# Four-layer residual block on one core: the next group's filters prepared across two superblocks, their root as a power on GpSimd

## The reference

```python
x = x + ddf(_gn(x))        # layer 0: decoupled dynamic 3x3 filter
x = x + v * sigmoid(q . mean(k))   # layer 1, on _gn(x)
x = x + conv3x3(_gn(x), ternary(weight)) + bias
x = x + softmax(Q^T K) V   # layer 3: attention over 3136 pixels, on _gn(x)
```

```python
sf = einsum('bchw,nc->bnhw', x, ws) + bs
sf = (sf - sf.mean(2)) / (sf.std(2, ddof=1) + 1e-10) * (GAIN / K)
out[c,i,j] = sum over taps of x[c,i+u,j+v] * cf[c,tap] * sf[tap,i,j]
```

## Time and profile before

| | us |
|---|---|
| median of 3 runs | 1942.02 (1940.48 to 1942.21) |
| the profiled execution | 1941.18 |
| its span, first to last instruction | 1939.4 |
| mean granted TensorE clock | 0.92 |

### The profile page before, as it was taken

One profiled execution on the slowest core, in us unless ns is written; L12 is line 12 of the kernel. 1 busy time (PEld: TensorE's weight loads), 2 busy tenths in 40 slices (PEclk: granted clock), 3 DMA queues, 4 the chain that ended last, 5 costly groups with the idle time before them and its releaser, 6 DMA issues.

```text
span 1939.4 us, 35957 instructions
## 1 busy us (share of the span) xinstructions
PE 1673.0 (86%) x10840; PEld 829.7 (43%) x10840; DVE 1257.6 (65%) x2446; ACT 1250.2 (64%) x2324; POOL 1098.9 (57%) x898
## 2 busy tenths in 40 slices
PE   5885899999887689999987859999999776999997
PEld 4362344444436234444443624444444452444442
DVE  5845777776574667777467466777748636777770
ACT  2035788888413578888831348888872335888885
POOL 3610477778651057777865006777787301677777
PEclk9996799999888689999998859999999796999998
DMA  2004000000000400000000040000000021000000
GB/s 81 0 1 83 1 7 6 6 6 6 12 0 1 83 1 6 6 6 6 11 7 1 2 82 2 6 6 6 11 6 5 0 32 19 1 6 11 6 6 10
DMA packets 8568, 26.91 MB, mean 14 GB/s; under 512 B 2256, under 2 KB 5840, under 8 KB 7888
## 3 DMA queue, kind: packets, MB, share of 16 engines
q1 hardware_dynamic: 8400, 24.79, 5.5%
HBM read 8.73 MB, written 6.42 MB: 8 GB/s over the span
## 4 chain that ended last, share of the span: by engine, by line
PE 50%; issue 16%; DVE 12%; POOL 10%; ACT 7%; SPq 3%; DMA 1%; POOLq 1%; ACTq 0%; DVEq 0%
PE PS L1202 20%; PE PS L1126 10%; PE PS L1158 9%; DVE nmt L642 4%; ACT PS L819 3%; SPq L369 3%; ACT Pb L862 2%; DVE nmt L635 2%; POOL accP L971 2%; POOL VT L928 2%; POOL VT L933 2%; POOL VT L930 2%; PE PS L1023 2%; PE PS L1111 2%; PE PS L1098 1%
## 5 line engine op out<-in xcount | busy, mean ns | idle before, releaser
L635 DVE TENSOR_REDUCE nmt<-PS 128x1 f32<-128x448 f32 x1176 | 680.3, 620 | 282.2 <-PE PS L1126 277.9
L971 POOL TENSOR_TENSOR accP<-accP,Pb 128x512 f32<-128x512 f32 (+1 forms) x532 | 677.9, 1274 | 167.3 <-ACT Pb L862 143.6
L862 ACT ACTIVATE Pb<-PS 128x896 f32<-128x896 f32 (+1 forms) x700 | 638.9, 914 | 132.0 <-PE PS L1158 107.1
L1202 PE MATMUL PS<-Pb,VT 128*64 128x448 f32 x2800 | 657.1, 549 | 4.4 <-ACT Pb L862 3.6
L1126 PE MATMUL PS<-Ka,Qa 96*64 96x448 bf16 x2744 | 514.2, 388 | 119.1 <-DMA Ka<-parts 57.7
L1158 PE MATMUL PS<-Qa,Ka 99*64 99x448 bf16 x2744 | 490.0, 358 | 5.3 <-ACT Qa L834 4.0
L819 ACT ACTIVATE PS<-PS,nmt 128x448 f32<-128x448 f32 x588 | 356.4, 606 | 120.0 <-DVE nmt L642 92.6
L1126 PEld LDWEIGHTS PS<-Ka,Qa 96*64 96x64 bf16 x2744 | 164.1, 115 | 421.7 <-issue 163.4
L1158 PEld LDWEIGHTS PS<-Qa,Ka 99*64 99x64 bf16 x2744 | 162.4, 111 | 249.5 <-issue 184.9
L1202 PEld LDWEIGHTS PS<-Pb,VT 128*64 128x64 f32 x2800 | 191.7, 138 | 95.7 <-ACT Pb L862 23.7
L964 POOL TENSOR_TENSOR accQ<-Pb 128x512 f32<-128x512 f32 x28 | 35.6, 1270 | 292.6 <-ACT Pb L862 292.6
(11 more groups left out here) (141 smaller groups left out, 1416.3 us busy)
## 6 DMA issues: line engine op xcount, KB each, us to landing
xin<-in_x SPq DMA_DIRECT2D x4, 1568.0 KB, 6.9
out<-xw SPq DMA_DIRECT2D x28, 224.0 KB, 1.9
Qa<-parts SPq DMA_DIRECT2D x48, 98.0 KB, 3.9
Ka<-parts SPq DMA_DIRECT2D x48, 98.0 KB, 4.1
wz<-in_weights SPq DMA_DIRECT2D x1, 829.0 KB, 8.2
cs<-in_cst SPq DMA_DIRECT2D x1, 576.0 KB, 8.8
wz<-in_weights SPq DMA_DIRECT2D x1, 576.0 KB, 9.6
cs<-in_cst SPq DMA_DIRECT2D x1, 256.0 KB, 6.3
```

The costliest lines, as they stand in the source:

```text
L635: nc.vector.reduce_max(nmt[:, target % 2, b, t:t + 1], PS[0:BLK, bank, 0:CH], X, negate=True).then_inc(mx_free, 1)
L862: nc.scalar.activation(Pb[0:r, j % PSLOTS, :, :], PS[0:r, 2 * (k % 2):2 * (k % 2) + 2, 0:CH], ACT.Exp).then_inc(exp_done, 1)
L971: nc.gpsimd.tensor_tensor((accQ if j < TO_ACCP else accP)[0:r, :, REST:CH], (accQ if j <= TO_ACCP else accP)[0:r, :, REST:CH], Pb[0:r, j % ...
L1202: last = mm(PS[C * h:C * h + C, OB, 0:CH], VT[:, j, C * h:C * h + C], Pb[:, j % PSLOTS, h, :], start=(j == 0), stop=(j == NQ - 1))
```

## The change

Five things are changed.

- `front_at` is called in superblocks 5 and 6, with j from -25 to 24 (0 is step 0 of superblock 6). The statistics' chunks go to steps 8 to 14 of superblock 5 (one a step, the aggregation with the last), mean and variance matmuls to steps 20 and 21, the power to 22, the bias to 23 (and with it the pooled vector), the normalisations to step 24 and steps 0 to 5, the spatial filter's matmuls to steps 1 to 7, variances 8, channel filter's matmuls 9, root 10, parts 11, centring 13, channel root 15, cf 16, transposes 17 to 22.
- `plan_banks` keeps banks 4 and 5 for the front from step 20 of superblock 5, and TensorE waits for the last maxima in them (`FRONT_LAST`).
- The square root of the per-pixel variances is a power 1/2 on GpSimd, 116 partitions x 56, and ScalarE's `front_root` is gone.
- The factor 1/8 of the variance is taken with the squares, and the refinement that followed the root on VectorE (four small instructions) is gone.
- GpSimd's superblock 5 is written out; its loop runs over superblocks 1 to 4.

```diff
-FRONT_XN = 7
-FRONT_SF = 8
-FRONT_TR = (20, 20, 21, 22, 23, 24, 24)
-FRONT_ROOT = 16
+FRONT_STATS = -17
+FRONT_MEAN = -5
+FRONT_XN = -1
+FRONT_SF = 1
+FRONT_TR = (17, 17, 18, 19, 20, 21, 22)
...
-        bank = min(free, key=lambda b: free[b][0])
+        bank = min((b for b in free if b not in front), key=lambda b: free[b][0])
...
+        if k == NQ * (NJ - 1) + FRONT_MEAN:
+            front = {b: free[b][1:] for b in (4, 5)}
...
-                link(g, nc.vector.tensor_tensor(sf2[:, :, :], sf[:, :, :], sf[:, :, :], ALU.mult))
+                link(g, nc.vector.scalar_tensor_tensor(out=sf2[:, :, :], in0=sf[:, :, :], scalar=1.0 / (TAPS - 1),
+                                                       in1=sf[:, :, :], op0=ALU.mult, op1=ALU.mult))
...
                 dve.wait_ge(sfsd_ready, g + 1)
-                link(g, nc.vector.tensor_scalar(sfs[:, 0, :], sfs[:, 4, :], 1e-30, None, ALU.add))
-                link(g, nc.vector.reciprocal(sfs[:, 1, :], sfs[:, 0, :]))
-                link(g, nc.vector.scalar_tensor_tensor(out=sfs[:, 3, :], in0=sfs[:, 2, :], scalar=0.5 / (TAPS - 1),
-                                                       in1=sfs[:, 1, :], op0=ALU.mult, op1=ALU.mult))
-                link(g, nc.vector.scalar_tensor_tensor(out=sfs[:, 5, :], in0=sfs[:, 4, :], scalar=0.5,
-                                                       in1=sfs[:, 3, :], op0=ALU.mult, op1=ALU.add))
-                link(g, nc.vector.tensor_scalar(sfs[:, 0, :], sfs[:, 5, :], 1e-10, None, ALU.add))
+                link(g, nc.vector.tensor_scalar(sfs[:, 0, :], sfs[:, 4, :], 1e-10, None, ALU.add))
...
-                    if j == 0:
-                        front_stats(g + 1)
+                    if FRONT_STATS <= j < FRONT_STATS + NJ:
+                        front_stats(g + 1, j - FRONT_STATS)
...
-                        if s == NJ - 1 and more:
-                            front_at(j)
+                        if s >= NJ - 2 and more:
+                            front_at(j - NQ * (NJ - 1 - s))
...
-            def front_root(g):
-                act.wait_ge(sfvar_ready, g + 1)
-                nc.scalar.activation(sfs[:, 4, :], sfs[:, 2, :], ACT.Sqrt, scale=1.0 / (TAPS - 1)).then_inc(sfsd_ready, 1)
...
+            def spatial_root(g):
+                pool.wait_ge(sfvar_ready, g + 1)
+                nc.gpsimd.tensor_tensor(sfs[:, 4, :], sfs[:, 2, :], phalf[0:SP2, :].to_broadcast([SP2, 2 * NSP]),
+                                        ALU.pow).then_inc(sfsd_ready, 1)
...
+                def front_at(j):
+
+                    if j == FRONT_MEAN + 2:
+                        power(g + 1, 0)
+                    elif j == FRONT_SF + NJ + 2:
+                        spatial_root(g + 1)
+                    elif j == FRONT_SF + NJ + 7:
+                        channel_root(g + 1)
...
-                    if j == 2:
+                    if j == FRONT_MEAN:
+                        wait_bank(FRONT_LAST[FB])
                         pair_mean(g + 1, 0, front)
...
-                    elif j == 7:
+                    elif j == FRONT_SF:
+                        wait_bank(FRONT_LAST[SFB])
                         front_mid(g + 1)
-                    elif j == 16:
+                    elif j == FRONT_SF + NJ + 1:
                         pe.wait_ge(recip, NJ * g + NJ)
                         front_channel_filter(g + 1)
```

More of the change, by code:

```diff
@@ L83, in plan_banks @@
 def plan_banks():
-    tiles, rows, dens = {}, {}, {}
+    tiles, rows, dens, front = {}, {}, {}, {}
     free = {4: (0.0, "nothing", 0), 5: (0.0, "nothing", 0), 7: (0.0, "nothing", 0)}
     def take(at, lasts, what, count):
-        bank = min(free, key=lambda b: free[b][0])
+        bank = min((b for b in free if b not in front), key=lambda b: free[b][0])
         last = free[bank][1:]
@@ L118, in plan_banks @@
             dens[s - 1] = take(k + 0.8, 1.5, "transposed", 2 * (s - 1) + 1)
+        if k == NQ * (NJ - 1) + FRONT_MEAN:
+            front = {b: free[b][1:] for b in (4, 5)}
         if j == ROWS_STEP:
             rows[s + 1] = take(k + 0.8, 2.5, "rows", s + 2)
-    return tiles, rows, dens
-TILES_AT, ROWS_BANK, DEN_BANK = plan_banks()
+    return tiles, rows, dens, front
+TILES_AT, ROWS_BANK, DEN_BANK, FRONT_LAST = plan_banks()
 COLS = {}
@@ L342, in build @@
         stored = sem("stored")
-        FRONT_LINKS, LINKS = 23, 31
+        FRONT_LINKS, LINKS = 19, 27
         block = ctx.enter_context(nc.Block())
@@ L465, in stats, with front_stats @@
                 bias(g, layer, small)
[L469 to L472, removed]
+            def front_stats(g, i):
+                if i == 0:
+                    n[0] = 0
+                    dve.wait_ge(x_loaded, 16 * g + 16)
+                if i < NJ - 1:
                     chunk_stats(xin, i)
-                mean_var(g, 0, chunk_stats(xin, NJ - 1))
+                else:
+                    mean_var(g, 0, chunk_stats(xin, NJ - 1))
             def front_bias(g):
@@ L678, in front_at @@
                 def front_at(j):
-                    if j == 0:
-                        front_stats(g + 1)
-                    elif j == 3:
+                    if FRONT_STATS <= j < FRONT_STATS + NJ:
+                        front_stats(g + 1, j - FRONT_STATS)
+                    elif j == FRONT_MEAN:
                         squares(g + 1, 0, front)
-                    elif j == 4:
+                    elif j == FRONT_MEAN + 1:
                         var_eps(g + 1, 0, front)
-                    elif j == 6:
+                    elif j == FRONT_MEAN + 3:
                         front_bias(g + 1)
-                    elif j == 8:
+                    elif j == FRONT_SF + 1:
                         front_mid(g + 1)
-                    elif j == 15:
+                    elif j == FRONT_SF + NJ:
                         front_sum_squares(g + 1)
-                    elif j == 18:
+                    elif j == FRONT_SF + NJ + 3:
                         front_parts(g + 1)
-                    elif j == 19:
+                    elif j == FRONT_SF + NJ + 5:
                         front_centre(g + 1)
-                    elif j == 22:
+                    elif j == FRONT_SF + NJ + 8:
                         front_channel_filter(g + 1)
@@ L701, in superblock @@
                     sidx = NJ * g + s
-                    if s == NJ - 1:
+                    if s == NJ - 2:
                         assert n[0] == LINKS, n[0]
                     for j in range(NQ):
-                        if s == NJ - 1 and more:
-                            front_at(j)
+                        if s >= NJ - 2 and more:
+                            front_at(j - NQ * (NJ - 1 - s))
                         for target, i, n_reduced, _, bank, _ in TILES_AT.get(NQ * s + j, ()):
@@ L723, in group @@
                 reciprocals(NJ * g + NJ - 1, 7)
-            front_stats(0)
+            for i in range(NJ):
+                front_stats(0, i)
             centre_weights()
@@ L886, in group @@
                     superblock(s)
[L887 to L890, removed]
                 copy_output(NJ * g + NJ - 1)
@@ L953, in finish, with superblock @@
                                             ALU.add).then_inc(fin_done, 1)
-                def superblock(sidx, s, first, front=False):
+                def front_at(j):
[5 more added lines that the diff above has]
+                        channel_root(g + 1)
+                def superblock(sidx, s, first, front=None):
                     for j in range(1, NQ):
[L957 to L960, removed]
+                        if front is not None:
+                            front_at(j + front)
                         r = key_rows(j)
@@ L977, in group @@
                 superblock(NJ * g, 0, True)
-                with pool.Fori(1, NJ - 1) as s:
+                with pool.Fori(1, NJ - 2) as s:
                     superblock(NJ * g + s, s, False)
-                superblock(NJ * g + NJ - 1, NJ - 1, False, more)
+                superblock(NJ * g + NJ - 2, NJ - 2, False, -NQ if more else None)
+                superblock(NJ * g + NJ - 1, NJ - 1, False, 0 if more else None)
                 finish(NJ * g + NJ - 1, NJ - 1)
             power(0, 0)
+            spatial_root(0)
             channel_root(0)
```

3 lines of the change are left out of this document (removed).

## The result

The changed kernel takes 1981.09 us (median of 4 runs, 1979.77 to 1982.03) beside 1942.05 for the kernel before in the same session: ratio 1.0204, interval 1.0191 to 1.0217. It is 39 us slower. The forecast was 1947.0 (+5) in a range of 1935 to 1985: the sign and the range held, the size was an eighth of what came.

What follows compares the result with a forecast made beforehand. TensorE was taken as nearly full where the front lies, with GpSimd's sums ending superblock 6. Per group 2.1 - 0.7 = +1.4, three times +4.2, prologue +0.8: +5.0 on 1941.18 gives 1946.2, plus 0.8 to the median 1947.0; range 1935 to 1985.

Steps and rivals of the forecast that it cites:

- T: Time of GpSimd's power on 116 x 56, the root in superblock 6 and the prologue: 2.1 us, bounds 0.67 and 21.5.
- 4T - 3.4: Whole-kernel change in us: three groups at T - 0.7 each, plus the prologue's T + 0.45 - 1.8.
- power by columns: Rival: the power takes 9 to 21.5 us, the Pb ring fills, ScalarE and TensorE stop; 1975 to 2025 us; chance 0.22.
- The forecast's own range: Whole kernel at 1943 to 1963 us, for a power of 1.2 to 6 us; chance 0.42.
- the geometric middle of the slopes: GpSimd's power: 29 ns per further column, chosen between the slopes of the low and high ends.
- the high end: GpSimd's power: 0.17 us fixed and 0.38 us for each of 56 columns, 21.5 us in all.
- GpSimd's path through superblock 6: GpSimd's root, channel root, ten sums, then the denominators end superblock 6 at 513.9 + T, later than TensorE's 513.8.
- Superblock 5: Loss of 1.0 us per group: 0.7 for statistics beside the maxima, 0.3 for mean and variance matmuls.
- Prologue: Nothing hides the root there: T + 0.45 replaces 1.8 us, +0.8 us at T = 2.1.
- the cheap-power rival: Power takes 0.67 us: change of -0.7, -3.7 or about -6.5 us, 1935.5 to 1941 us; chance 0.30.
- the 2.5 us freed on TensorE: Superblock 6: without table loads and Sqrt, TensorE's 0.85 us idle and 1.7 us of low clock go.

Runs made afterwards that it cites:

- fourteen: Changed kernel with GpSimd's power on 14 of the 56 pixel columns, standard deviation left at 1.0 for the others: 1955.22 us, ratio 1.0072 to the kernel before.
- The kernel with one column: Changed kernel with GpSimd's power on 1 of the 56 pixel columns, standard deviation left at 1.0 for the others: 1942.95 us, ratio 1.0010 to the kernel before.
- the power alone: Kernel before, its placement kept, with ScalarE's Sqrt at step 16 replaced by GpSimd's power and no refinement: 1979.1 us, ratio 1.0195.

## Why the prediction was right in its sign and wrong in its size

**The path was right, and the rival came.** With T = 9.27 the prediction's own 4T - 3.4 gives +33.7; measured +39.0. That was the second rival, "power by columns", with its mechanism: ring of Pb full, ScalarE and TensorE stop, clock falls behind them. It was given 0.22. The forecast's own range, 1943 to 1963 for T from 1.2 to 6, did not hold; the outer range held because it was drawn over this rival, and 9.27 lies at the rival's low end. The formula is too low at every width: -1.2, +7.0 and +33.7 for one, fourteen and all columns, measured +1.2, +13.5 and +39.0.

**The mis-sized term is T**: 2.1 forecast, 9.27 measured. The bounds, 0.67 and 21.5, held it. (The upper one is a little low: GpSimd's fixed part by the earlier trace rows is 1134 - 448 x 2.2 = 148 ns, not 170, which gives 22.6.) The choice between them failed. I took the geometric middle of the slopes (29 ns a column) because it was "nearer to the row of one column"; the slope is 159. The 0.55 us of one column were read as mostly fixed cost. 0.39 of them are fixed, and 0.16 are the column itself, not 0.38 as in the high end. A row with one column can't split the two, and each of the 56 columns multiplies the mistake: 0.16 x 56 = 8.9 us. The rule of the Trainium skill (GPSIMD Engine Reference, "Performance versus the Vector engine"), 2.6 cycles an element, holds for the addition (2.2 ns), and the power measured 159 ns, 72 times as much. The rule on dependent chains on the same page ("Performance pitfalls for Q7 kernels") pointed to the side that came: at 4 cycles of 1.2 GHz a step, an estimate from the page, 159 ns would be a chain of 48 dependent steps. No run here shows what the power is made of.

**GpSimd's path through superblock 6** came out term by term. From the superblock's start: root begins at 22.5 (forecast 490.1 - 467.3 = 22.8); from its end to the end of the channel root 10.25 (9.6); ten sums 13.4 (13.5); denominators 1.1 (0.7, since they ran at 1.2 GHz). The 0.65 too little in the second term are the wait, 2.40 against 1.4: VectorE's addition took 1.25, not the 0.2 that I had kept, and the multiply at L526 1.26 for 0.68.

**Superblock 5**: 1.0 forecast, 1.5 measured. Statistics 0.40 for 0.7, mean and variance matmuls 0.64 for 0.3; 0.44 for the normalisation at its last step was missing, as I had looked for that cost in superblock 6 alone.

**Prologue**: T + 0.45 - 1.8 gives 7.9, measured 7.8.

**What the formula lacked.** Of the 7.0 us between its 33.7 and the 40.7 of the spans, superblock 6 holds 1.9 and superblock 5 1.5. The other 3.6 lie where the change edits nothing: the way from first tap to first exponential (3.4 over three groups) and group 3's superblock 0 (1.5, the clock of its first 7 us), less the 1.4 of the gaps ahead of the first taps. Of the 3.4, 0.7 in group 1 and 0.95 in group 2 are there by VectorE's ninth product, 9 us behind the first tap; the clock of group 1's second 7 us is 0.93, before 1.00. The rest is explained by no run here.

**The moved front earned nothing**: the cheap-power rival had put its worth at T = 0.67 to -0.7 us and down to -6.5. The kernel with one column (T 0.55) was at +1.2. The two table loads went, as forecast, and with them the stop behind them; a longer one came in its place (4.11 us, then a clock of 0.51). That the 2.5 us freed on TensorE were worth nothing because GpSimd's sums end the superblock fits the stages; no run changes the table loads alone.

## What to carry to other kernels

A price read from an instruction of one column says nothing of the price per column; where a change multiplies the columns by 56, treat the whole instruction as possibly per-column and forecast toward that end, above all for an operation that is more than an addition. Before work is moved to another engine, look at the end of the stage: TensorE's denominators started 0.05 us behind GpSimd's last sum already, so GpSimd had no room behind its channel root; and its 3.92 us of idle earlier in the superblock hid none of the power, since the power alone cost all of T. And a VectorE duration has to be read from a row with the same neighbours: 0.22 us becomes 1.3 beside GpSimd's sums.

## What the runs showed of the hardware

- GpSimd's power costs 0.39 us + 159 ns per column (1, 14 and 56 columns: 0.549, 2.592, 9.274 us). Its addition costs 2.2 ns per column.
- VectorE instructions with two SBUF operands, and fp32 copies or additions of a constant in SBUF, wait for a sum of GpSimd's that already runs: 0.22 became 1.17 to 1.32, 0.19 became 1.25, 0.42 became 1.38, 0.68 became 1.26 to 1.63. With one operand in PSUM they took 0.68 or 0.69 in both places. Reductions (116x504, 0.68) and reciprocals (116x56, 0.50) from SBUF kept their time beside sums. The sums beside them stretch from 1.27 to as much as 1.71. The Trainium skill (VectorE: DVE Perf Modes, "Rules for kernel authors") gives two ways for a matmul's output: operate on it in PSUM, or copy it to SBUF first if many operations follow. For the second way the prologue speaks (cast 0.42 from SBUF, 0.68 from PSUM); inside the loop, beside GpSimd, it is the other way round (1.38 against 0.68).
- After TensorE idled 4.11 us, 6.3 us of work ran at 0.51 of the clock; after 3.29 and 2.75 us with little between, 7 us at 0.50. Superblock 0 takes 1.5 us more where its first 7 us run at 0.50 than where they run at 0.70.
